# Picking the query rows of each pair of sequences by matrix products instead of by a copy between partitions

## The chip, the core and the metric

The kernel runs on one core of a Trainium2 chip. The metric is the device time of one execution in microseconds (us). The core has a matrix engine (TensorE: PE for products, PEld for its weight loads), VectorE (DVE), ScalarE (ACT), GpSimd (POOL), and queues that issue transfers (DMA), of which SyncE's is SP.

## The reference

A decoder layer for 16 sequences of 56 tokens with 512 features:

```python
x = layernorm(x + mixer(x))              # a state-space mixer: 128 heads of 64, 8 groups
x = layernorm(x + xattn(x, ctx_4096))    # e = softmax(x @ ctx^T); e @ ctx, 1500 keys of 512 per sequence
x = layernorm(x + ffn(x))                # x @ W_base.T + b, and two of eight low-rank experts
```

Only the second and third lines concern us. `xattn` has no projections: the queries are the rows of the first layer norm's output, and the context serves as keys and as values. All of it is in float32.

## The kernel before

The 896 tokens lie packed in `acc`, seven tiles of 128 rows: tile t holds tokens 128t to 128t+127. Up to about 1185 us the mixer runs, group by group. Then comes the attention, which goes by pairs of sequences (`PAIRS` = 8, counted from 0). A pair owns 112 tokens, 112u to 112u+111, which mostly straddle two tiles of `acc`. On the chip a pair is laid out padded: the first sequence on rows 0 to 55, the second on rows 64 to 119, the rows between unused.

The copy `load_x1(u)` (lines 475 to 487, POOL queue) makes that layout: two or three transfers from `acc` into `x1p`, a tile with two slots, whose gaps were zeroed once. `turn_queries(u)` on PE (line 1285) waits for these transfers, transposes the four blocks of 128 features of `x1p` into the PSUM bank `turn` (bank 4) and signals `q_tr`. ACT copies `turn` into `qT` in sixteen pieces (`queries`, line 712). Pair 0 doesn't wait for its transfer: `turn_first_queries` multiplies tile 0 of `acc` by `spread`, an identity with a gap between columns 56 and 64 (line 1298). `x1p` is also the residual that VectorE adds at the end of the pair (`norm2_sum`, line 1036).

I call pass u what PE does in the last loop for u = 0 to 7. In order:

- `score(u)` (line 1392): the products of queries and transposed keys
- `turn_x2(u-1)` (line 1436): transposes of the previous pair's output, which ACT then copies (`x2_evac`, line 724)
- `turn_queries(u+1)` (line 1289)
- `feed_forward(u-1)` (lines 1444 and 1448), which waits for `x2_evac`
- `turn_probs(u)` (line 1463): transposes of the probabilities, which waits for ACT's exponential (line 730)
- `values(u, 0..2)` (line 1477), with `turn_hw` and `lora` (lines 1453, 1457) of the previous pair between them

On DVE a pass has the key transposes of the next pair (`keys_part`, line 934, twelve of them, the first two ahead of `score_max(u)`, line 1022), the routing of the experts and the layer norms. On ACT it has `x2_evac`, `probs_exp`, `router_exp`, eight pieces of `queries(u+1)`, the copies of two thirds of the transposed probabilities into `probsT` (line 736), and the other eight pieces. Each engine executes its list strictly in this order. The context (6 MB per pair) comes through the SP queue into a ring of six units (line 350). A unit is reloaded once the values that read it are done.

`probs` and `probsT` are two tiles of the same shape. `probs_exp(u)` already waits for `z2_done`, that is, for the end of the values of the pair before.

Of the kernel before, what the change touches and what calls it, by code (L numbers as in the profile page):

```python
# [15 lines left out]
f32 = mybir.dt.float32  # L16
f32r = mybir.dt.float32r
ALU = mybir.AluOpType
# [3 lines left out]
P = 128  # L22
# [34 lines left out]
def layer_kernel(nc, A):  # L57
    ctx = ExitStack()
    with ctx:
        def sb(name, shape, dt=f32, stack=ctx):  # L60
            return stack.enter_context(nc.sbuf_tensor(name, shape, dt))
# [8 lines left out]
        acc = sb("acc", [P, TT, DM])  # L70
        ident = sb("ident", [P, P])
        ones = sb("ones", [P, SUB])
# [53 lines left out]
        sq_last = sb("sq_last", [P, TOK], f32, mix)  # L126
        spread = sb("spread", [P, P], f32, mix)
        ssq = sb("ssq", [P, TT], f32, mix)
# [12 lines left out]
        probs = sb("probs", [P, KJ, P], f32, att)  # L141
        probsT = sb("probsT", [P, KJ, P], f32, att)
        x2 = sb("x2", [P, 2, DM], f32, att)
# [14 lines left out]
        for n, k in widths.items():  # L158
# [26 lines left out]
            ss_done ss_picked ss_summed ms_done rg_done outa_done outa_evac outb_done psum_added sum_done  # L185
            wo_high wo_low zeroed y_low_last q0_part spread_set
            residual_loaded residual_set ln1_step ln1_pool ln1_var ln1_rstd x1_set ffn_loaded x1p_zero
# [65 lines left out]
        def x1_landed(u):  # L253

            return 16 * sum(x1_pieces(k) for k in range(u % 2, u + 1, 2))
# [123 lines left out]
        def _(pool):  # L379
            g_ = nc.gpsimd  # L380
            g_.memset(ones[:], 1.0)
            g_.memset(epsc[:], -0.5)
            g_.memset(ident[:], 0.0).then_inc(s["pool_step"], 1)
            g_.memset(causal[:], 1.0)
            g_.memset(causal_hi[:], 1.0).then_inc(s["pool_step"], 1)
            pool.wait_ge(s["pool_step"], 2)
            g_.affine_select(out=ident[:], in_=ident[:], compare_op=ALU.not_equal, fill=1.0, base=0,
                             pattern=[[-1, P]], channel_multiplier=1)
# [4 lines left out]
            last.then_inc(s["consts_set"], 1)  # L393
            g_.memset(spread[:], 0.0).then_inc(s["pool_step"], 1)
            pool.wait_ge(s["consts_set"], 1)
            pool.wait_ge(s["pool_step"], 3)
            for q in range(2):
                last = g_.tensor_copy(spread[:, PAD * q:PAD * q + LEN], ident[:, LEN * q:LEN * (q + 1)])
            last.then_inc(s["spread_set"], 1)
            g_.memset(decay[:].rearrange("p a n -> p (a n)"), 0.0)  # L400
# [361 lines left out]
        def _(dve):  # L762
# [176 lines left out]
            dve.wait_ge(s["zeroed"], 1)  # L939
            v.tensor_reduce(own[:], ident[:].rearrange("p (i a) -> p a i", a=SUB), AX.X, ALU.add)  # L940
            v.tensor_copy(causal[PAD:P, :], causal_hi[PAD:P, :]).then_inc(s["dstep"], 1)
# [49 lines left out]
            keys_part(0, 0, 1)  # L991
            group_squares(GROUPS)
            last_halves(0)
            last_sum(0)
# [156 lines left out]
        def _(pe):  # L1151
# [3 lines left out]
            for k in range(KT):  # L1155
                for r, n in ((0, 4), (1, 3)):
                    i = 2 * k + r
                    for q in range(n):
                        t = 4 * r + q
                        pe.wait_ge(s["h_scaled"], t + 1)  # L1160
                        last = tr([proj[0], proj[1], yt, ob][i // 2][:, i % 2, q * P:(q + 1) * P],
                                  part[:, t, k * P:(k + 1) * P], ident[:])
                    last.then_inc(s["hT_done"], 1)
# [18 lines left out]
            def dt_token_major():  # L1182
                pe.wait_ge(s["dt_dve"], 6)
                for i in range(4):
                    for q in range(4):
                        pair = 4 * (i % 2) + q
                        last = tr([yt, ob][i // 2][:, i % 2, q * P:(q + 1) * P],
                                  (cs_all, dt_all)[i // 2][:, pair * P:(pair + 1) * P], ident[:])
                    last.then_inc(s["cst_done"], 1)
# [5 lines left out]
            def transpose_hid(g, c):  # L1195
                if not within(g, c):
                    return

                wait(pe, s["silu_done"], 10, g, c + 3 if c >= 0 else c + 1)
                wait(pe, s["yres_done"], CT, g, c)  # L1200
                for r in range(2):
                    for q in range(4):
                        pair = 4 * r + q
                        last = tr(yt[:, r, q * P:(q + 1) * P], hid[:, c % 2, pair * P:(pair + 1) * P], ident[:])  # L1204
                    last.then_inc(s["t_done"], 1)
# [178 lines left out]
            last_part(6, 7).then_inc(s["outb_done"], 1)  # L1384
            turn_first_queries()

# [43 lines left out]
            def turn_x2(u):  # L1430
                pe.wait_ge(s["x2_done"], u + 1)
                if u == 0:
                    pe.wait_ge(s["psum_added"], GROUPS * TT)
                at_least(pe, s["hw_evac"], u)
                for k in range(KT):
                    last = tr(misc[:, k * P:(k + 1) * P], x2[:, u % 2, k * P:(k + 1) * P], ident[:])
                last.then_inc(s["x2_tr"], 1)
# [13 lines left out]
            def turn_hw(u):  # L1451
                pe.wait_ge(s["hw_done"], u + 1)
                tr(misc[:, 0:P], hw, ident[:]).then_inc(s["hw_tr"], 1)

# [4 lines left out]
            def turn_probs(u, r):  # L1459
                if r == 0:  # L1460
                    pe.wait_ge(s["exps_done"], u + 1)
                for j in range(KB):
                    last = tr(bank[:, r, j * P:(j + 1) * P], probs[:, KB * r + j, :], ident[:])
                last.then_inc(s["pT_tr"], 1)
# [102 lines left out]
```

## Time and profile before

| | us |
|---|---|
| median of 3 runs | 1479.44 (1477.43 to 1480.03) |
| the profiled execution | 1479.15 |
| its span in the trace | 1477.4 |

| engine | busy us | share of the span |
|---|---|---|
| PE | 1420.3 | 96% |
| PEld | 1169.2 | 79% |
| DVE | 993.2 | 67% |
| ACT | 752.2 | 51% |
| POOL | 496.0 | 34% |

The trace counts from the span's start. Between the two times of the profiled execution lie 1.75 us around the span. Busy shares are means over stages: the mixer fills about four fifths of the span, the attention the last 290 us. Matmuls are pipelined, so the end of one overlaps the start of the next. A float32 product appears as two MATMUL and two LDWEIGHTS records, a transpose as one of each. "[0.51 <-DMA x1p<-acc]" behind a row means that the engine was idle for 0.51 us before it and that this transfer ended the idle time.

### The profile page before, as it was taken

How to read it: one execution, taken by the hardware profiler on the slowest of the kernel's cores; microseconds unless marked ns; L12 is line 12 of the kernel's file. 1: busy time of each engine (PE TensorE's matmuls, PEld its weight loads, DVE VectorE, ACT ScalarE, POOL GpSimd, SP SyncE). 2: the span in 40 equal slices, each digit the busy share in tenths (PEclk: the TensorE clock that was granted, in tenths of full speed). 3: DMA queues.
4: the chain of work that ended last, by engine and by line, in shares of the span. 5: the costliest groups of instructions: out<-in, count | busy, mean ns of one | idle time of the engine just before them, and what ended most of it. 6: DMA issues, size and time to landing. Idle time of an engine off the chain costs nothing.

```text
span 1477.4 us, 30164 instructions
## 1 busy us (share of the span) xinstructions
PE 1420.3 (96%) x12816; PEld 1169.2 (79%) x12816; DVE 993.2 (67%) x1313; ACT 752.2 (51%) x1003; POOL 496.0 (34%) x368
## 2 busy tenths in 40 slices
PE   5899999999999999999999999999999978999995
PEld 4798989898989888888888888889888864445442
DVE  5784768476847684767476757765775676888764
ACT  5765636463756274636463656365536443543340
POOL 5253435242524253425342434333433320111101
PEclk9999999999999999999999999999999999999998
DMA  4431213121312131213221312221221365566610
GB/s 150 118 106 54 82 51 99 47 90 47 98 58 88 40 98 58 81 45 100 65 74 53 97 55 73 58 91 55 73 65 55 131 240 195 217 242 261 195 44 13
DMA packets 53347, 142.60 MB, mean 97 GB/s; under 512 B 9777, under 2 KB 9905, under 8 KB 46951
## 3 DMA queue, kind: packets, MB, share of 16 engines
q1 hardware_dynamic: 51518, 137.01, 28.3%
q0 software_dynamic: 1696, 3.67, 0.8%
q8 instruction: 101, 1.65, 0.5%
q14 instruction: 32, 0.26, 0.0%
HBM read 136.53 MB, written 2.29 MB: 94 GB/s over the span
## 4 chain that ended last, share of the span: by engine, by line
PE 83%; DVE 7%; issue 4%; DMA 3%; ACT 1%; POOL 1%; SPq 0%; DVEq 0%; POOLq 0%; ACTq 0%
PE bank L1174 47%; PE bank L1242 20%; PE bank L1217 5%; PE bank L1204 4%; DVE keysT L934 3%; DMA x1p<-acc 2%; PE bank L1477 2%; PE bank L1392 2%; PE bank L1448 1%; DMA ring_a<-in_context 1%; PE bank L1274 1%; DVE conv L809 1%; PE bank L1229 1%; PE bank L1444 0%; DVE part L770 0%
## 5 line engine op out<-in xcount | busy, mean ns | idle before, releaser
L1174 PE MATMUL bank<-h_hi,w_hi 128*128 128x448 f32 x1152 | 338.2, 375 | 2.2 <-DVE conv L809 2.2
L432 POOL TENSOR_TENSOR y_lo<-yg,y_hi 128x896 fp32r<-128x896 f32 x63 | 134.2, 2129 | 578.6 <-ACT y_hi L605 538.5
L1174 PE MATMUL bank<-h_lo,w_hi 128*128 128x448 f32 x1152 | 328.0, 366 | 0.0
L1174 PE MATMUL bank<-h_hi,w_lo 128*128 128x448 f32 x1152 | 327.1, 365 | 0.0
L809 DVE SCALAR_TENSOR_TENSOR conv<-bank,conv_w,conv 128x880 f32<-128x880 f32 (+2 forms) x240 | 268.0, 1117 | 85.6 <-ACT conv L578 79.8
L1174 PEld LDWEIGHTS bank<-h_hi,w_lo 128*128 128x128 f32 x1152 | 216.8, 188 | 17.4
L1174 PEld LDWEIGHTS bank<-h_lo,w_hi 128*128 128x128 f32 x1152 | 216.9, 188 | 17.2
L416 POOL TENSOR_TENSOR w_lo<-w_raw,w_hi 128x512 fp32r<-128x512 f32 x144 | 188.3, 1308 | 119.1 <-ACT w_hi L544 117.6
L1174 PEld LDWEIGHTS bank<-h_hi,w_hi 128*128 128x128 f32 x1152 | 208.2, 188 | 20.1 <-DVE conv L809 2.6
L854 DVE TENSOR_TENSOR hd_dt<-bank,dt_j 128x512 f32<-128x512 f32 x128 | 82.4, 685 | 208.0 <-PE bank L1204 208.0
L1242 PE MATMUL bank<-wo_hi,y_hi 128*128 128x512 f32 x420 | 165.2, 393 | 0.0
L605 ACT ACTIVATE y_hi<-yg 128x896 fp32r<-128x896 f32 x64 | 60.9, 951 | 203.0 <-DVE yg L836 202.7
L1242 PE MATMUL bank<-wo_lo,y_hi 128*128 128x512 f32 x420 | 163.7, 390 | 0.0
L1242 PE MATMUL bank<-wo_hi,y_lo 128*128 128x512 f32 x420 | 163.4, 389 | 0.0
L585 ACT ACTIVATE hid<-conv 128x896 f32<-128x896 f32 x64 | 61.0, 953 | 150.2 <-DVE conv L809 150.0
L439 POOL TENSOR_TENSOR sqsum<-sq,sqsum 128x896 f32<-128x896 f32 x54 | 115.2, 2133 | 0.0
L578 ACT ACTIVATE conv<-bank,conv_b,conv_w 128x896 f32<-128x896 f32 x80 | 87.1, 1089 | 31.9 <-PE bank L1174 31.7
L1392 PE MATMUL bank<-keysT,qT 32*64 32x384 f32 (+5 forms) x2304 | 90.2, 457 | 9.8 <-issue 6.3
L1242 PEld LDWEIGHTS bank<-wo_hi,y_hi 128*128 128x128 f32 x420 | 78.8, 188 | 19.1 <-issue 2.5
L1242 PEld LDWEIGHTS bank<-wo_hi,y_lo 128*128 128x128 f32 x420 | 78.9, 188 | 16.6
L1392 PEld LDWEIGHTS bank<-keysT,qT 32*64 32x64 f32 x2304 | 59.1, 137 | 41.6 <-issue 27.5
L1242 PEld LDWEIGHTS bank<-wo_lo,y_hi 128*128 128x128 f32 x420 | 78.9, 188 | 15.8
(181 smaller groups left out, 1932.1 us busy)
## 6 DMA issues: line engine op xcount, KB each, us to landing
w_raw<-in_w_in SPq DMA_DIRECT2D x144, 256.0 KB, 2.8
decay<-cs_scratch SPq DMA_DIRECT2D x128, 196.0 KB
ring_a<-in_context SPq DMA_DIRECT2D x24, 1024.0 KB, 7.9
ring_b<-in_context SPq DMA_DIRECT2D x21, 1024.0 KB
wo_raw<-in_w_out SPq DMA_DIRECT2D x64, 256.0 KB, 2.6
ring_b<-in_context SPq DMA_DIRECT2D x3, 896.0 KB
acc<-in_x SPq DMA_DIRECT2D x1, 1792.0 KB, 8.5
out<-z POOLq DMA_DIRECT2D x16, 112.0 KB, 2.7
```

The source lines that it names most:

```text
L416: g_.tensor_tensor(w_lo[:, slot, :], w_raw[:, slot, :], w_hi[:, slot, :].bitcast(f32), ALU.subtract).then_inc(s["w_low"], 1)
L432: g_.tensor_tensor(y_lo[:, c % 4, :], yg[:, c % 2, :], y_hi[:, c % 4, :].bitcast(f32), ALU.subtract).then_inc(s["y_low"], 1)
L439: g_.tensor_tensor(out=sqsum[:], in0=sq[:], in1=sqsum[:], op=ALU.add).then_inc(s["sqsum_done"], 1)
L578: a(seqs(conv[:, m % 2, :]), bank_seqs(proj[idx % 2]), ACT.Identity, bias=conv_b[:, bass.ds(col, 1)], scale=conv_w[:, bass.ds(col, 1), TAP ...
L585: a(real(dst), seqs(conv[:, m % 2, :]), ACT.Silu).then_inc(s["silu_done"], 1)
L605: a(y_hi[:, c % 4, :], yg[:, c % 2, :], ACT.Copy).then_inc(s["y_high"], 1)
L809: v.scalar_tensor_tensor(out=dst[:, :, sh:LEN], in0=src[:, :, 0:LEN - sh], scalar=conv_w[:, bass.ds(col, 1), TAPS - 1 - sh], in1=dst[:, :, ...
L854: v.tensor_tensor(hd_dt[:, 4 * r:4 * r + 4, :].rearrange("p q (h d) -> p q h d", h=2), yt[:, r, :].rearrange("p (q h d) -> p q h d", q=4, ...
L1174: last = mm(place, w[:, k * P:(k + 1) * P], x[:, k, half * HALF:(half + 1) * HALF], start=(k == 0 and i == 0), stop=(k == KT - 1 and i == 2))
L1217: last = mm(yt[HD * h:HD * (h + 1), b, pair * PAD:pair * PAD + LEN], hd_dt[own_rows, pair, HD * h:HD * (h + 1)], mixw[own_rows, h, pair, : ...
L1242: last = mm(ob[:, b, :], y[:, c, tok], w[:, c, :], start=(c == 0 and i == 0), stop=(c == 3 and i == 2))
L1392: last = mm(scores[PAD * q:PAD * (q + 1), row, :].rearrange("p (j i) -> p j i", i=SQ)[:, j0:j1, 0:n], qT[lo:lo + SQ, b // 4, b % 4, PAD * ...
```

## The change

The queries of every pair are now made as those of pair 0 were: by products of the tiles of `acc` with 0/1 columns. A wide tile `shifted` holds zeros with the identity in columns 128 to 255. A strip of 112 of its columns that starts 128 + 112u - 128t columns in picks, from tile t, the rows that belong to pair u. A pair that straddles two tiles (pairs 1 to 6) needs two products per block of features, summed in PSUM; pairs 0 and 7 need one. The output goes to columns 0 to 55 and 64 to 119 of each block of `turn`, and the columns between are zeroed once by VectorE. PE waits for `x1_set` (the tiles' layer norm) and no longer for the transfers. The transfers stay, for the residual. `spread` goes away, and `ident` becomes a slice of `shifted`. `probsT` becomes another name for `probs`, so that the transposed probabilities overwrite those that they were made from.

```diff
-        ident = sb("ident", [P, P])
+        shifted = sb("shifted", [P, 2 * P + 2 * LEN])
+        ident = shifted[:, P:2 * P]
...
-        spread = sb("spread", [P, P], f32, mix)
...
-        probsT = sb("probsT", [P, KJ, P], f32, att)
+        probsT = probs
...
-            g_.memset(ident[:], 0.0).then_inc(s["pool_step"], 1)
+            g_.memset(shifted[:], 0.0).then_inc(s["pool_step"], 1)
...
-            g_.memset(spread[:], 0.0).then_inc(s["pool_step"], 1)
-            pool.wait_ge(s["consts_set"], 1)
-            pool.wait_ge(s["pool_step"], 3)
-            for q in range(2):
-                last = g_.tensor_copy(spread[:, PAD * q:PAD * q + LEN], ident[:, LEN * q:LEN * (q + 1)])
-            last.then_inc(s["spread_set"], 1)
...
             group_squares(GROUPS)
+            v.memset(turn.rearrange("p (a i) -> p a i", i=PAD)[:, :, LEN:PAD], 0.0).then_inc(s["turn_zero"], 1)
             last_halves(0)
...
             def turn_queries(u):
-                pe.wait_ge(x1_loaded[u % 2], x1_landed(u))
-                pe.wait_ge(s["q_set"], u)
+                first, end = 2 * LEN * u, 2 * LEN * (u + 1)
+                tiles = range(first // P, (end - 1) // P + 1)
+                pe.wait_ge(s["x1_set"], tiles[-1] + 1)
+                at_least(pe, s["q_set"], u)
+                if u == 0:
+                    pe.wait_ge(s["turn_zero"], 1)
                 for k in range(KT):
-                    last = tr(turn[:, k * P:(k + 1) * P], x1p[:, u % 2, k * P:(k + 1) * P], ident[:])
-                last.then_inc(s["q_tr"], 1)
-
-            def turn_first_queries():
-                pe.wait_ge(s["x1_set"], 1)
-                pe.wait_ge(s["ss_picked"], GROUPS)
-                pe.wait_ge(s["spread_set"], 1)
-                for k in range(KT):
-                    last = mm(turn[:, k * P:(k + 1) * P], acc[:, 0, k * P:(k + 1) * P], spread[:],
-                              start=True, stop=True)
+                    place = turn[:, k * P:(k + 1) * P].rearrange("p (q i) -> p q i", i=PAD)[:, :, 0:LEN]
+                    for t in tiles:
+                        at = P + first - t * P
+                        last = mm(place, acc[:, t, k * P:(k + 1) * P],
+                                  shifted[:, at:at + 2 * LEN].rearrange("p (q i) -> p q i", i=LEN),
+                                  start=(t == tiles[0]), stop=(t == tiles[-1]))
                 last.then_inc(s["q_tr"], 1)
...
-            turn_first_queries()
+            turn_queries(0)
```

## Rows read from the trace of the kernel before

**Rows 1.** Page, part 4: the chain that ended last, by engine and line.
```profile
PE 83%; DVE 7%; issue 4%; DMA 3%; ACT 1%; POOL 1%; SPq 0%; DVEq 0%; POOLq 0%; ACTq 0%
```

**Rows 2.** What waited for tile x1p, from its own view: us, times.
```profile
  PE bank L1289: 7.5, 6
```

**Rows 3.** Timeline of pass 4: start, length, engine, line, what, idle before.
```profile
1342.03 0.42 PEld L1436 LDWEIGHTS bank<-ident,x 128*128 128x128 f32 x4 [0.60 <-issue]
...
1342.73 0.60 ACT L724 ACTIVATE x2T<-bank 128x512 f32<-128x512 f32 x1 [7.93 <-PE bank L1436]
1343.32 0.42 PEld L1289 LDWEIGHTS bank<-ident,x1p 128*128 128x128 f32 x4 [0.87 <-DMA x1p<-acc]
...
1343.71 1.00 PEld L1444 LDWEIGHTS bank<-waT,x2T 128*128 128x128 f32 x8
...
1343.96 1.54 ACT L730 ACTIVATE probs<-bank,smalls 128x1536 f32<-128x1536 f32 x1 [0.64 <-DVE smalls L1022]
...
1348.18 1.47 PE L1463 MATMUL bank<-ident,probs 128*128 128x128 f32 x12
```

**Rows 4.** Timeline, weight loads of `turn_queries` in passes 2, 3, 5 and 6.
```profile
1282.85 0.42 PEld L1289 LDWEIGHTS bank<-ident,x1p 128*128 128x128 f32 x4 [0.51 <-DMA x1p<-acc]
...
1313.00 0.42 PEld L1289 LDWEIGHTS bank<-ident,x1p 128*128 128x128 f32 x4 [0.84 <-DMA x1p<-acc]
...
1373.16 0.42 PEld L1289 LDWEIGHTS bank<-ident,x1p 128*128 128x128 f32 x4 [0.68 <-DMA x1p<-acc]
...
1406.06 0.42 PEld L1289 LDWEIGHTS bank<-ident,x1p 128*128 128x128 f32 x4 [1.86 <-DMA x1p<-acc]
```

**Rows 5.** Timeline of pass 6, then of pass 7, which turns no queries.
```profile
1403.77 0.42 PEld L1436 LDWEIGHTS bank<-ident,x 128*128 128x128 f32 x4 [0.60 <-issue]
...
1406.44 1.00 PEld L1444 LDWEIGHTS bank<-waT,x2T 128*128 128x128 f32 x8
...
1434.80 0.65 PE L1436 MATMUL bank<-ident,x 128*128 128x128 f32 x4
...
1436.14 1.19 PE L1444 MATMUL bank<-waT,x2T 128*128 128x136 f32 x8 [0.69 <-ACT x2T L724]
```

**Rows 6.** Timeline: the products that pick pair 0's queries.
```profile
1193.67 1.05 PE L1298 MATMUL bank<-spread,acc 128*128 128x128 f32 x8
```

**Rows 7.** Timeline of pass 1.
```profile
1243.94 0.66 PE L1436 MATMUL bank<-ident,x 128*128 128x128 f32 x4
...
1248.49 1.11 PE L1289 MATMUL bank<-ident,x1p 128*128 128x128 f32 x4 [3.90 <-DMA x1p<-acc]
...
1250.63 2.37 DVE L934 STREAM_TRANSPOSE keysT<-ring_a 128x1024 f32<-128x1024 f32 x2 [12.24 <-DMA ring_a<-in_context]
...
1254.68 1.54 ACT L730 ACTIVATE probs<-bank,smalls 128x1536 f32<-128x1536 f32 x1 [9.45 <-DVE smalls L1022]
...
1256.37 1.54 PE L1463 MATMUL bank<-ident,probs 128*128 128x128 f32 x12 [0.40 <-ACT probs L730]
...
1262.01 3.65 PE L1477 MATMUL bank<-ring_b,probsT 125*64 125x512 f32 x16 [0.42 <-ACT probsT L736]
```

**Rows 8.** PE by stretches of pass 1: length, busy (x), granted clock, DMA share, GB/s.
```profile
1244.60:1248.50 3.90, 0.01 (x1) 0.77 1.02 333
1248.50:1253.50 5.00, 5.00 (x15) 0.50 1.01 418
1253.50:1256.00 2.50, 2.48 (x6) 0.99 1.01 413
```

**Rows 9.** The same view for the idle stretch of pass 0.
```profile
1218.20:1221.00 2.80, 0.00 (x0) 1.00 0.00 0
```

**Rows 10.** Timeline around the added VectorE memset: a like one, and the idle time that covers it.
```profile
1189.54 0.75 DVE L923 SCALAR_TENSOR_TENSOR acc<-part,rg,acc 128x512 f32<-128x512 f32 x1 [1.06 <-POOL rg L444]
...
1193.36 0.09 DVE L999 MEMSET bank<- 128x36 f32 x1
```

**Rows 11.** Timeline of the start: PE's first work.
```profile
11.86 1.57 PE L1161 MATMUL bank<-ident,part 128*128 128x128 f32 x4 [11.86 <-DVE part L770]
```

More of the change, by code:

```diff
@@ L185, in layer_kernel @@
             ss_done ss_picked ss_summed ms_done rg_done outa_done outa_evac outb_done psum_added sum_done
-            wo_high wo_low zeroed y_low_last q0_part spread_set
+            wo_high wo_low zeroed y_low_last q0_part turn_zero
             residual_loaded residual_set ln1_step ln1_pool ln1_var ln1_rstd x1_set ffn_loaded x1p_zero
@@ L386, in _ @@
             pool.wait_ge(s["pool_step"], 2)
-            g_.affine_select(out=ident[:], in_=ident[:], compare_op=ALU.not_equal, fill=1.0, base=0,
+            g_.affine_select(out=ident, in_=ident, compare_op=ALU.not_equal, fill=1.0, base=0,
                              pattern=[[-1, P]], channel_multiplier=1)
@@ L939, in _ @@
             dve.wait_ge(s["zeroed"], 1)
-            v.tensor_reduce(own[:], ident[:].rearrange("p (i a) -> p a i", a=SUB), AX.X, ALU.add)
+            v.tensor_reduce(own[:], ident.rearrange("p (i a) -> p a i", a=SUB), AX.X, ALU.add)
             v.tensor_copy(causal[PAD:P, :], causal_hi[PAD:P, :]).then_inc(s["dstep"], 1)
@@ L1161, in _ @@
                         last = tr([proj[0], proj[1], yt, ob][i // 2][:, i % 2, q * P:(q + 1) * P],
-                                  part[:, t, k * P:(k + 1) * P], ident[:])
+                                  part[:, t, k * P:(k + 1) * P], ident)
                     last.then_inc(s["hT_done"], 1)
@@ L1187, in dt_token_major @@
                         last = tr([yt, ob][i // 2][:, i % 2, q * P:(q + 1) * P],
-                                  (cs_all, dt_all)[i // 2][:, pair * P:(pair + 1) * P], ident[:])
+                                  (cs_all, dt_all)[i // 2][:, pair * P:(pair + 1) * P], ident)
                     last.then_inc(s["cst_done"], 1)
@@ L1203, in transpose_hid @@
                         pair = 4 * r + q
-                        last = tr(yt[:, r, q * P:(q + 1) * P], hid[:, c % 2, pair * P:(pair + 1) * P], ident[:])
+                        last = tr(yt[:, r, q * P:(q + 1) * P], hid[:, c % 2, pair * P:(pair + 1) * P], ident)
                     last.then_inc(s["t_done"], 1)
@@ L1435, in turn_x2 @@
                 for k in range(KT):
-                    last = tr(misc[:, k * P:(k + 1) * P], x2[:, u % 2, k * P:(k + 1) * P], ident[:])
+                    last = tr(misc[:, k * P:(k + 1) * P], x2[:, u % 2, k * P:(k + 1) * P], ident)
                 last.then_inc(s["x2_tr"], 1)
@@ L1452, in turn_hw @@
                 pe.wait_ge(s["hw_done"], u + 1)
-                tr(misc[:, 0:P], hw, ident[:]).then_inc(s["hw_tr"], 1)
+                tr(misc[:, 0:P], hw, ident).then_inc(s["hw_tr"], 1)
             def lora(u):
@@ L1462, in turn_probs @@
                 for j in range(KB):
-                    last = tr(bank[:, r, j * P:(j + 1) * P], probs[:, KB * r + j, :], ident[:])
+                    last = tr(bank[:, r, j * P:(j + 1) * P], probs[:, KB * r + j, :], ident)
                 last.then_inc(s["pT_tr"], 1)
```

## The prediction

> **What bounds the kernel now.** I read the page's chain first: 83% of the time that sets the end is PE and 3% are transfers [rows 1]. So a microsecond added to PE's list is likely to show, and the transfers can give back little. Next I asked the view of tile x1p who waits for the copy that the change takes out of PE's way. PE waits 7.5 us in all, six times [rows 2]. That is the most the removed wait can return. The timeline shows where the six waits lie: 3.90 us in pass 1 [rows 7], 0.5 to 0.9 us in each of passes 2 to 5 [rows 3, 4], 1.86 us in pass 6 [rows 4]. (The idle times of the weight loader are slightly longer than those of the products, and I use them, since the load comes first.) The transfer itself takes some 7 us, but the scores of the pass, about 10.6 us, run beside it. Only its tail is seen.
>
> Then comes the question for each wait: what is late next once it is gone? It has three different answers, so I take the passes apart.
>
> **A product's price.** The old turn is four transposes. From its first weight load to the first of the feed-forward it takes 0.39 us (1343.32 to 1343.71 in pass 4, [rows 3]). The new turn of a straddling pair is 8 float32 products, each with two records, so 16. The nearest row is the pick of pair 0, the same operation with 128 columns: 8 records in 1.05 us, of which the last one takes 0.275 us, so they start (1.05 - 0.275)/7 = 0.111 us apart [rows 6]. With 112 columns I scale by 112/128 to 0.097. 16 records take 1.6 us (0.100 each, with a little for the strided output). The bounds are 16 x 0.0955 = 1.53 if only the columns count, and 16 x 0.111 = 1.78 if the weight load sets the pace, which doesn't shrink with the columns.
>
> The Trainium skill speaks against the change here. "TensorE: Matmul & The Clock Gate", section "Terms", says that the transpose mode makes float32 four times faster. The trace disagrees: the twelve transposes of the probabilities take 1.47 us, that is (1.47 - 0.27)/11 = 0.109 us each [rows 3], against 0.222 us for a product [rows 6], a factor of two. By the page, a product of 112 columns would take 4 x 0.109 x 7/8 = 0.38 us and eight of them 3.05 us. What that would give stands under the first rival.
>
> **Passes 2 to 5: slower.** PE is the path here. The probabilities' transposes start right behind the feed-forward, without idle time, and the exponential that they need was done 2.7 us before, at 1345.5 [rows 3]. VectorE and ACT wait for PE in these passes. The turn and the wait before it cost 0.39 + idle: with 0.51, 0.84, 0.87 and 0.68 us idle [rows 3, 4] that is 0.90, 1.23, 1.26 and 1.07. The new turn takes 1.6 each time and needs nothing that is late: its tiles' norms were finished a pass or more before. The differences are +0.70, +0.37, +0.34 and +0.53, in sum **+1.9 us** (+1.7 at 1.53, +2.7 at 1.78). Less than nothing is excluded, because the feed-forward also waits for ACT's copy of x2 (1342.73 + 0.60 [rows 3]), 1.34 us after the transposes of x2 start. The products cover all of that, so there is no gain beyond what I counted.
>
> **Pass 6: faster.** It turns pair 7, which lies in one tile: 4 products, 0.8 us. From the transposes of x2 to the feed-forward it took 1406.44 - 1403.77 = 2.67 us. Pass 7, which turns nothing, shows what is late next: 1436.14 - 1434.80 = 1.34 us, set by ACT's copy [rows 5]. 0.42 + 0.8 fits under it. The gain is **-1.3 us**. The later work of that pass is PE's alone, so I keep it whole (bounds -1.3 and 0).
>
> **Pass 1: no gain, and probably a loss.** PE waited 3.90 us for x1p, but afterwards it waits again, for the exponential, at 1256.37. The exponential follows the row maximum, which on VectorE stands behind the first key transposes of the next pair, and these waited 12.24 us for the context's transfer, until 1250.63 [rows 7]. The change moves none of that. PE finishes earlier and waits longer: turn at 1244.36, +1.6, feed-forward 4.47 us as in pass 4 (1343.71 to 1348.18 [rows 3]), end at 1250.4. Then it is idle 5.9 us at a stretch, where there were 3.9 and later 0.4.
>
> What an idle spell costs is in the clock. After the 3.9 us idle spell the granted clock was 0.50 (1.2 of 2.4 GHz) for the next 5.0 us of work, then full again; 0.77 within the spell means that it fell 1.8 us before the work resumed, 6.8 us in all [rows 8]. Before, this slow stretch lay on work that had time, ahead of the wait for the exponential. Now the idle spell lies right ahead of work that has none. 5.0 us at half speed do 2.5 us of work too little. The second part of the values stood idle for ACT for 0.42 us [rows 7], which absorbs as much: 2.5 - 0.4 gives **+2.1 us**. The bounds are 0, if the clock holds, and 6.8/2 - 0.4 = 3.0, if the whole slow stretch falls on this work. A gain is excluded by VectorE's order. The rule of the skill's same page, section "Why this matters for your kernels", is that an idle gap between bursts of products drops the array to half its clock. Here the trace agrees (0.50 after 3.9 us).
>
> **The rest, costed at nothing.** Pass 0: the turn of pair 1 is 1.1 us longer, ahead of an idle stretch of 2.8 us [rows 9]. Without that cover it would be +1.1. Pair 0's pick has 112 columns instead of 128, 0.1 us less, and the scores behind it wait for key transposes anyway. VectorE's memset of 64 columns (like one of 36, 0.09 us) stands ahead of `last_halves(0)`, and what follows that idles 1.06 us for POOL [rows 10]. Uncovered it would cost 0.1. At the start POOL clears 368 columns instead of 128, and PE starts only at 11.86, for VectorE [rows 11]. Only a clearing that takes microseconds longer would be seen. POOL's memset and two copies of `spread` go, ahead of a wait that POOL has anyway. The single buffer for the probabilities adds no wait: each third is overwritten after its own transposes, for which the copies waited already, and the next exponential waited already for the end of the values. The new waits of PE (`x1_set`, `turn_zero`) have the whole PE list queued behind them, but are set long before: `turn_zero` some 5 us before the pick, since VectorE is past it at 1189.54 [rows 10].
>
> **Sum.** 1.9 - 1.3 + 2.1 = +2.7 us on the profiled execution's 1479.15 gives **1481.9 us** (1481.85). That execution is 0.29 us below the median of 1479.44, so against the median it is +2.4 us, 0.16%. A measurement of this kernel tells about 0.2%, 3.0 us, from no change. The forecast's own range is 1479.15 + 0 + 1.7 - 1.3 = 1479.5 to 1479.15 + 3.0 + 2.7 - 1.3 = 1483.6, or 1484.9 without the gain of pass 6.
>
> **Rivals.**
> - *Products at the price of their weight load (slower).* If a record takes about 0.19 us, the turn takes 3.05 us. This happens if loads of different contents don't overlap the products when these are short. Passes 2 to 5 then cost 12.2 - 4.46 = +7.7, pass 6 gains only 2.67 - (0.42 + 1.5) = 0.7, pass 1 stays at +2.1: 1488.3 us. The sum passes 0.2% from 0.105 us a record (4 x 16 x 0.105 - 4.46 - 1.3 + 2.1 = 3.1); up to 0.111 that is the forecast's own upper half, beyond it this rival. Against it stands the 0.111 of the same operation [rows 6]. For it stands that no row has fewer than 128 columns with full weights of this type. It is also the time that the skill's factor of four gives.
> - *Pass 1's wait was real (faster).* If the context for pair 2 usually lands before about 1247, the exponential is ready when PE is, and the 3.9 us count. The sum is 1.9 - 1.3 - 3.9 = -3.3, 1475.9 us. Against it: the transfer landed at 1250.63 with the DMA share at 1.0 [rows 7, 8], and VectorE would have to gain 4 us.
> - *The clock holds in pass 1 (no change).* After 2.8 us idle in pass 0 the clock stayed at 1.00 [rows 9]. Where it holds, only 1.9 - 1.3 = +0.6 is left: 1479.8 us. Against it: 5.9 us idle is twice that and longer than the 3.9 that brought it down [rows 8].
>
> **How the numbers follow.** Forecast 0.6; of this 0.38 within 0.2% and 0.22 above, since 1482.1 is within its range. Load price 0.08, slower. Real wait 0.1, faster. Clock holds 0.2, of which 0.18 is within 0.2% and 0.02 slower. The last 0.02 is any other gain or loss, half each. Faster 0.11, same 0.56, slower 0.33. The range leaves out most of the faster and of the load-price case and holds the rest with its bounds: 1477.5 to 1486.0.
>
> **What would show it.** In the changed kernel's timeline: in passes 2 to 5 some 1.6 us of picking products and no idle time before them (a longer turn: first rival); 2.0 us from x2's transposes to the feed-forward, against 1.34 to 1.68; in pass 6, 1.34; in pass 1 an idle PE from about 1250.4 to 1256.4 with the exponential as releaser, and a granted clock of 0.50 after it (1.00: third rival; no idle time: second). The forecast is wrong if the passes are no longer bound by PE, or if stalls inside the scores move.

## The result and the profile after

| | before | after |
|---|---|---|
| median of 12 runs | 1479.40 us (1475.14 to 1480.79) | 1483.16 us (1481.86 to 1486.81) |
| ratio, 95% interval | 1 | 1.003 (1.0022 to 1.0038) |
| profiled execution, and its span | 1479.15, 1477.4 | 1483.10, 1481.4 |
| PE's share of the chain | 83% [rows 1] | 91% |
| PE waits for the copy x1p | 7.5 us, 6 times [rows 2] | not at all |

The change makes the kernel 3.8 us slower. The forecast was 1481.9, within 1477.5 to 1486.0. The time lies in the range and 1.3 us above the forecast, and by its interval it is slower rather than "no change", which had the higher chance (0.56 against 0.33). Much of the work below asks which terms of the sum were right and what the 1.3 us are.

The chain of the changed kernel, from its page, against [rows 1]: PE has 8 points more, DVE 3 fewer, the transfers and "issue" 2 fewer each.

```profile
PE 91%; DVE 4%; issue 2%; DMA 1%; ACT 1%; POOL 0%; SPq 0%; DVEq 0%; ACTq 0%
```

Pass 4 of the changed kernel in the timeline (start, length, engine, line, what, idle before), against [rows 3]:

```profile
1344.84 0.66 PE L1431 MATMUL bank<-shifted,x 128*128 128x128 f32 x4
1345.34 1.94 PE L1292 MATMUL bank<-shifted,acc 128*128 128x112 f32 x16
1345.54 0.60 ACT L718 ACTIVATE x2T<-bank 128x512 f32<-128x512 f32 x1 [8.11 <-PE bank L1431]
1347.11 1.11 PE L1439 MATMUL bank<-waT,x2T 128*128 128x136 f32 x8
```

The wait is gone. In its place stand 16 product records. ACT's copy of x2 is done at 1345.54 + 0.60 = 1346.14, so the feed-forward at 1347.11 waits for the products and for nothing else. It starts 2.27 us after the transposes of x2 instead of 1.79. The 16 records take 1.77 us of the chain (start, length, what):

```profile
1345.50 1.77 PE bank L1292 x16
```

Pass 6 of the changed kernel, against [rows 5]. Eight records stand there, and then a stall that waits for no semaphore:

```profile
1406.03 0.66 PE L1431 MATMUL bank<-shifted,x 128*128 128x128 f32 x4
1406.52 1.04 PE L1292 MATMUL bank<-shifted,acc 128*128 128x112 f32 x8
1406.72 0.60 ACT L718 ACTIVATE x2T<-bank 128x512 f32<-128x512 f32 x1 [16.43 <-PE bank L1431]
1409.12 1.09 PE L1439 MATMUL bank<-waT,x2T 128*128 128x136 f32 x8 [1.56 <-issue]
```

Pass 1 of the changed kernel, against [rows 7]:

```profile
1248.00 0.93 PE L1292 MATMUL bank<-shifted,acc 128*128 128x112 f32 x7 [0.89 <-issue]
...
1249.71 3.60 PE L1443 MATMUL bank<-wbT,x2T 128*128 128x512 f32 x8
...
1251.15 2.37 DVE L928 STREAM_TRANSPOSE keysT<-ring_a 128x1024 f32<-128x1024 f32 x2 [11.23 <-DMA ring_a<-in_context]
...
1255.20 1.54 ACT L724 ACTIVATE probs<-bank,smalls 128x1536 f32<-128x1536 f32 x1 [8.44 <-DVE smalls L1017]
...
1256.88 2.82 PE L1458 MATMUL bank<-shifted,probs 128*128 128x128 f32 x12 [3.58 <-ACT probs L724]
```

and PE by stretches of it (length, busy (x), granted clock, DMA share, GB/s), against [rows 8]:

```profile
1253.30:1256.80 3.50, 0.00 (x1) 0.80 1.00 417
1256.90:1261.80 4.90, 4.90 (x18) 0.50 0.55 226
1262.40:1266.00 3.60, 3.60 (x20) 1.00 0.22 32
```

VectorE's key transposes still wait for the context and the exponential still follows them, so PE's wait of 3.9 us became a wait of 3.6 us further down. The clock that it brings down, 0.50 for 4.9 us, now meets the transposes of the probabilities: 2.82 us instead of 1.54. Before, it met the feed-forward, which had time [rows 7, 8].

The 4.0 us between the two profiled executions, stage by stage. For the passes the numbers are from one start of x2's transposes to the next:

| stage | after - before, us |
|---|---|
| mixer, up to the pick of pair 0 (1193.7 to 1194.5) | +0.8 |
| pass 0, up to the x2 transposes of pass 1 (1243.94 to 1245.47) | +0.7 |
| pass 1 (37.98 to 37.86) | -0.1 |
| passes 2, 3, 4 (29.82, 30.29, 30.04 to 30.53, 30.98, 30.66) | +2.0 |
| pass 5 (31.70 to 30.53) | -1.2 |
| pass 6 (31.03 to 31.34) | +0.3 |
| pass 7 (22.18, both) | 0 |
| behind the last transposes of x2 (20.4 to 21.85) | +1.4 |

One pair of profiles misleads in places, which is why the experiments follow. The last row is the slow stretch of the clock. It comes from the 2.92 us wait ahead of the last x2 transposes, which both kernels have. The tail is 21.7 us in the kernel with only the wait removed (experiment 1, the old turn) and 20.5 in a second profile of the changed kernel (experiment 5), so it varies from profile to profile and belongs to neither. Pass 0's 0.7 us look like that too: after the idle spell ahead of the first scores the same 221 records take 7.98 us before and 8.90 after. But in experiment 5 they take 7.98 and pass 0 is still 0.85 us longer than before, so this row isn't explained. The same eight instructions of the last pair's feed-forward, before and then after:

```profile
1460.30 4.33 PE L1448 MATMUL bank<-wbT,x2T 128*128 128x512 f32 x8
```
```profile
1462.87 5.68 PE L1443 MATMUL bank<-wbT,x2T 128*128 128x512 f32 x8
```

### The profile page after: what moved, and what is told of

Same layout as the page of the kernel before. It is cut to its first block, busy times and chain, and to the rows that moved or that the text cites. A ratio compares the mean times of both kernels' runs of the same rounds, so it can differ in the third digit from the quotient of the medians.

```text
span 1481.4 us, 30313 instructions
## 1 busy us (share of the span) xinstructions
PE 1432.0 (97%) x12892; PEld 1179.2 (80%) x12892; DVE 993.0 (67%) x1314; ACT 753.2 (51%) x1003; POOL 496.1 (33%) x365
## 4 chain that ended last, share of the span: by engine, by line
PE 91%; DVE 4%; issue 2%; DMA 1%; ACT 1%; POOL 0%; SPq 0%; DVEq 0%; ACTq 0%
PE bank L1169 47%; PE bank L1237 20%; PE bank L1387 5%; PE bank L1472 5%; PE bank L1212 5%; PE bank L1199 4%; PE bank L1443 2%; DMA ring_a<-in_context 1%; DVE keysT L928 1%; PE bank L1269 1%; PE bank L1458 1%; DVE conv L803 1%; PE bank L1439 1%; PE bank L1292 1%; PE bank L1224 1%
```

## The experiments

All ratios are against the kernel before on the same chip, with 95% intervals. "x2 to feed-forward" is the time on PE from the start of x2's transposes to the start of the feed-forward, in passes 2 to 5.

**1. The wait alone, without products (`e1_no_wait`).** The kernel before, whose turn transposes a tile of `acc` that is ready, so the queries of the pairs are other rows than they should be. x1p is still loaded. This prices the wait that the change removes.

```diff
-                pe.wait_ge(x1_loaded[u % 2], x1_landed(u))
+                tile = min(u, TT - 1)
+                pe.wait_ge(s["x1_set"], tile + 1)
...
-                    last = tr(turn[:, k * P:(k + 1) * P], x1p[:, u % 2, k * P:(k + 1) * P], ident[:])
+                    last = tr(turn[:, k * P:(k + 1) * P], acc[:, tile, k * P:(k + 1) * P], ident[:])
```

> The kernel before, but the turn of pairs 1 to 7 transposes a tile of acc instead of x1p, so PE has no transfer to wait for and still pays the old 0.39 us for the turn. (The queries of these pairs are other rows than the reference's.) This is the removed wait alone. Theory: passes 2 to 5 fall to the 1.34 us that ACT's copy of x2 sets (0, -0.3, -0.3, -0.1), pass 6 gains 1.3 us, and pass 1 loses about 1.9 us, because its idle spell moves to just ahead of the probabilities' transposes and they and the first values run at a granted clock of 0.50. Sum -0.2 us, ratio 0.9999. Rival 'pass 1's wait was real': -6 us, ratio 0.996. Rival 'the clock in pass 1 costs nothing': -2.1 us, ratio 0.9986.

Measured: 1478.05 us, 0.9989 (0.9978 to 1.0). Of 7.5 us of waiting, 1.1 us came back, and the interval just reaches "nothing". x2 to feed-forward is 1.35 us (before: 1.43, 1.76, 1.79, 1.58), in pass 6 1.34. In pass 1 it is 1.34 too, instead of 5.46, and that gain is gone by the exponential. Its timeline:

```profile
1246.11 1.19 PE L1445 MATMUL bank<-waT,x2T 128*128 128x136 f32 x8 [0.25 <-ACT x2T L724]
...
1256.03 2.82 PE L1464 MATMUL bank<-ident,probs 128*128 128x128 f32 x12 [5.30 <-ACT probs L730]
```

and its stretch behind that (length, busy (x), granted clock, DMA share, GB/s):

```profile
1256.10:1260.90 4.80, 4.80 (x18) 0.50 0.47 196
```

So pass 1's wait was covered, and its removal costs by the clock, products or not. From the end of the exponential to the scores of pass 2 it is 14.28 us before, 16.10 after and 16.23 here.

**2. The products behind the old wait (`e2_products_after_wait`).** The changed kernel, whose products also wait for the copy, as the transposes did. x1p is loaded in the changed kernel anyway.

```diff
+                if u:
+                    pe.wait_ge(x1_loaded[u % 2], x1_landed(u))
```

> The changed kernel, but PE again waits for the transfer of x1p before the products. This is the price of the products alone. Theory: 1.77 us for a straddling pair instead of 0.39 in passes 2 to 5 (+5.5 us), +0.5 us in pass 6, and in pass 1 about +2 us, since 16 records at half clock end after the exponential is ready. Sum about +8 us against the kernel before, ratio 1.0054. Rival 'the products cost little, and what the changed kernel lost lies in stalls elsewhere': +2 to +4 us, ratio 1.002.

Measured: 1487.59 us, 1.0054 (1.0034 to 1.0074). x2 to feed-forward is 2.81, 3.28, 2.95 and 2.99 us, against 2.27, 2.26, 2.27 and 2.26 without the wait. With the wait kept, the change costs 8.5 us, without it 3.8 and 4.9 (the changed kernel and experiment 5), so removing the wait returns some 4 us of what the rest of the change costs. PE doesn't read x1p in this kernel, so the profile puts its six waits for the copy down to "issue" (8.4 us in all). In pass 1 the products run beside the slow clock: 16 of them take 3.73 us. The probabilities' transposes then follow without idle time:

```profile
1250.28 3.73 PE L1294 MATMUL bank<-shifted,acc 128*128 128x112 f32 x16 [3.87 <-issue]
...
1258.97 1.47 PE L1460 MATMUL bank<-shifted,probs 128*128 128x128 f32 x12
```

**3. The single buffer for the probabilities, alone (`e3_one_buffer`).**

```diff
-        probsT = sb("probsT", [P, KJ, P], f32, att)
+        probsT = probs
```

> The kernel before with one buffer for the probabilities and nothing else. Theory: every wait that it needs was there already, so nothing changes: ratio 1.000, within 0.15%, and the same length of passes 2 to 5 (29.8 to 30.3 us, 31.7 with a stall). Rival 'reading and overwriting the same tile costs': some 0.5 us a pass, +4 us, ratio 1.0027.

Measured: 1480.74 us, 1.0007 (0.9997 to 1.0016). The interval holds 1, and no new wait stands in its passes. It costs nothing that can be told.

**4. The same wait removed another way: the transfer issued earlier (`e4_issue_first`).** The kernel before. POOL issues the load of x1p ahead of the norm of the pair before instead of behind it.

```diff
-                if u >= 1:
-                    rstd2(u - 1)
                 if 1 <= u < PAIRS - 1:
                     load_x1(u + 1)
+                if u >= 1:
+                    rstd2(u - 1)
```

> The kernel before, but POOL issues the transfer of x1p for the next pair ahead of the power for the second layer norm, not behind it, about 1.7 us earlier. Transposes and transfer stay. Theory: the waits of passes 2 to 5 (0.5 to 0.9 us) go down to what ACT's copy of x2 needs, pass 6 gains up to 1.3 us, pass 1 gains nothing: -2.1 us, ratio 0.9986. Rival 'the landing follows the context's traffic and not the issue': less than 1 us, ratio 0.9995 to 1.000.

Measured: 1478.57 us, 0.9993 (0.9984 to 1.0002). The waits all but go: x2 to feed-forward is 1.35, 1.34, 1.64, 1.35, in pass 6 1.34, in pass 1 1.42. Everything that the removal of the wait can bring is in this edit, without one product. The total doesn't tell from no change.

**5. The changed kernel again (`e5_after_again`), for a second profile.**

> The changed kernel once more, beside the next one. Theory: ratio 1.0025 to 1.003. A second profile tells which parts of the first one's passes repeat: 30.5 to 31.0 us for passes 2 to 5, about 16 us from the probabilities' transposes of pass 1 to the scores of pass 2 (14.1 in the kernel before), and PE's stalls of 0.9 and 1.6 us that the profile puts down to issue.

Measured: 1484.08 us, 1.0037 (1.0024 to 1.005). From the end of pass 1's exponential to the scores of pass 2 it is 15.15 us, between the 14.28 of before and the 16.10 of the first profile. x2 to feed-forward is 2.26 or 2.27 in each of passes 2 to 5, and stalls without a semaphore stand again in passes 1 and 6 (1.45 and 1.84 us). Passes 5 and 6 take 31.17 and 31.62 us. The idle spell ahead of the probabilities' transposes of pass 1 is 3.18 us here.

**6. Keeping PE busy in pass 1's idle spell, six products (`e6_fill_idle`).** The changed kernel. Products whose result nobody reads stand between the feed-forward and the wait for the exponential.

```diff
+                if u == 1:
+                    pe.wait_ge(s["z2_done"], 1)
+                    for _ in range(6):
+                        mm(pv, shifted[:, P:2 * P], acc[:, 0, :], start=True, stop=True)
```

> The changed kernel with six float32 products of 512 columns (0.43 us each, result unused) between the feed-forward and the probabilities' transposes of pass 1, so that TensorE works through most of the spell in which it waits for the exponential. Theory (the clock's fall behind the moved idle spell costs 1.9 us): granted clock 1.00 after it, 14.1 us from those transposes to the scores of pass 2, and 1.9 us less in all than the changed kernel, ratio 1.0015 to the kernel before. Rival (the clock there costs nothing, pass 1 is longer for another reason): as the changed kernel, 1.0028, or more by whatever the added products delay.

Measured: 1483.6 us, 1.0036 (1.0022 to 1.005). I had mis-sized the filling: a float32 product of 512 columns is two records, 0.86 us and not 0.43. The twelve records ran past the end of the exponential and pushed the transposes back by 1.35 us. But these then ran at full speed:

```profile
1252.34 5.31 PE L1491 MATMUL bank<-acc,shifted 128*128 128x512 f32 x12
...
1257.49 1.47 PE L1458 MATMUL bank<-shifted,probs 128*128 128x128 f32 x12
```

From the end of the exponential to the scores it is 14.74 us, 1.35 of them the overshoot.

**7. Products of half the columns (`e7_56_columns`).** The changed kernel, which picks only the first sequence of each pair; the queries of the second one are zero. If columns set the price of a product, this one falls.

```diff
...
-                    place = turn[:, k * P:(k + 1) * P].rearrange("p (q i) -> p q i", i=PAD)[:, :, 0:LEN]
+                    place = turn[:, k * P:(k + 1) * P].rearrange("p (q i) -> p q i", i=PAD)[:, 0:1, 0:LEN]
...
-                                  shifted[:, at:at + 2 * LEN].rearrange("p (q i) -> p q i", i=LEN),
+                                  shifted[:, at:at + LEN].rearrange("p (q i) -> p q i", i=LEN),
...
```

> The changed kernel, but the picking products have 56 moving columns instead of 112 and fill only the first sequence of each pair. (The second sequence's queries are zero.) Row 'weight load sets the pace': the records stay 0.11 us apart and the turn of a straddling pair stays 1.77 us. Row 'columns set the pace': about 0.05 us apart and 0.8 us.

Measured, in a single run: 1483.28 us. The chain of pass 4:

```profile
1343.98 1.73 PE bank L1292 x16
```

1.73 us for 16 records, against 1.77 with 112 columns: 0.108 against 0.111 each. Half the columns take 2% off. It isn't the moving columns that set the pace.

**8. The early transfer with three spells filled (`e8_early_transfer_filled`).** Experiment 4, with unused products of 512 columns ahead of the first scores (7), in pass 1 (9) and ahead of the last x2 transposes (6).

```diff
+            def fill(place, n):
+                for _ in range(n):
+                    mm(place, ident[:], acc[:, 0, :], start=True, stop=True)
...
+                fill(bank[:, 0, :], 7)
...
+                if u == 1:
+                    pe.wait_ge(s["z2_done"], 1)
+                    fill(pv, 9)
...
+            pe.wait_ge(s["pT_evac0"], PAIRS)
+            fill(bank[:, 0, :], 6)
```

> The kernel before with the transfer issued first (as in the earlier run) and unused float32 products of 512 columns in three idle spells of TensorE: seven ahead of pair 0's scores, nine ahead of the probabilities' transposes of pass 1, six ahead of the last pair's transposes of x2. Theory (idle spells cost through the clock behind them): -0.8, -0.6 and -1.8 us for the spells and -1 to -2 for the earlier transfer, ratio 0.9965. Rival (the clock behind idle spells lies on work that has time): only what the earlier transfer gives, 0.9993.

Measured: 1481.26 us, 1.0018 (1.0009 to 1.0027). This carried the same error in size: the fillings take 6.17, 7.89 and 5.31 us, and each one runs past what PE would have waited for. It says nothing against filling, only what filling too much costs.

**9 and 10. The place in memory (`e9_before_moved`, `e10_after_moved`).** The profiles had shown something that no theory of mine held: all kernels built on the changed one reach the pick of pair 0 some 2 us later than experiments 1, 3 and 4, although nothing in the mixer is changed. What differs is where its tiles lie. The strips make a tile ahead of them 960 bytes wider in each partition. So one kernel is the one of experiment 3 with such a gap (its `probsT = probs` isn't repeated in the cut), the other the changed kernel with 64 bytes more, 1024 in all.

```diff
         ident = sb("ident", [P, P])
+        gap = sb("gap", [P, 2 * P + 2 * LEN - P])
```
```diff
         ident = shifted[:, P:2 * P]
+        gap = sb("gap", [P, 16])
```

> The kernel before with one buffer for the probabilities and an unused tile of 240 columns behind ident, so that every tile of the mixer lies 960 bytes further on, as in the changed kernel. No instruction differs from the one-buffer run. In all five profiles of kernels with the changed kernel's code a group of the mixer takes 144.85 us, in the others 144.5 us. Theory (the tiles' place in memory does it): 144.85 us a group here too, the picks of pair 0 at 1194 to 1195 us instead of 1192.5, ratio 1.002. Rival (something in the changed kernel's instructions does it, the identity as a slice of a wider tile among them): 144.5 us a group, ratio 1.0005.

> The changed kernel with an unused tile of 16 columns behind the wide identity, so that the mixer's tiles lie 1024 bytes further on than before instead of 960. Theory of place, if multiples of 1024 bytes count alike: 144.5 us a group, 2.3 us less than the changed kernel, ratio 1.001 to 1.0015. Rival: 144.85 us a group and ratio 1.003, as the changed kernel; then either the distance that counts is another or the place does not count, which the run before this one tells.

Measured: 1480.88 us, 1.0008 (0.9999 to 1.0017), and 1483.7 us, 1.0021 (1.0011 to 1.0031). The total that the theory gave for the first, 1.002, lies above its interval; the second's interval holds both of its expectations. The mixer's period is the time between two starts of its first product of a group. In the timelines, first experiment 3, then the same with the gap of 960 bytes:

```profile
467.22 1.15 PE L1229 MATMUL bank<-cmat,bmat 128*64 128x56 f32 x32
...
611.77 1.15 PE L1229 MATMUL bank<-cmat,bmat 128*64 128x56 f32 x32
```
```profile
468.03 1.15 PE L1230 MATMUL bank<-cmat,bmat 128*64 128x56 f32 x32
...
612.87 1.15 PE L1230 MATMUL bank<-cmat,bmat 128*64 128x56 f32 x32
```

144.55 us and 144.84. Then the changed kernel, and the changed kernel with 1024 bytes instead of 960:

```profile
467.95 1.15 PE L1224 MATMUL bank<-cmat,bmat 128*64 128x56 f32 x32
...
612.79 1.15 PE L1224 MATMUL bank<-cmat,bmat 128*64 128x56 f32 x32
```
```profile
466.78 1.15 PE L1225 MATMUL bank<-cmat,bmat 128*64 128x56 f32 x32
...
611.32 1.15 PE L1225 MATMUL bank<-cmat,bmat 128*64 128x56 f32 x32
```

144.84 us and 144.54. The gap alone slows the mixer of the kernel without the change, and 64 bytes more undo it in the changed one. Up to the end of the mixer that is some 2.0 to 2.5 us: pair 0 is picked at 1192.5 in experiment 3, 1194.5 with the gap, 1194.5 in the changed kernel, 1192.0 with 1024 bytes. The kernel before was picked at 1193.7 only because its first group began 1.5 us late in the profiled execution, so the table above shows 0.8 where other pairs of profiles show about 2. The chain over one group says which products are slower, the kernel of experiment 3 first, then with the gap:

```profile
602.11 9.73 PE bank L1174 x48
```
```profile
603.02 9.92 PE bank L1175 x48
```

Two of a group's 18 projections stand in this piece. They and one more take 0.4133 us for each two records instead of 0.4055, the others don't change. The slower mixer is shown by the period, which is 144.5 to 144.6 in all seven profiles without the 960 bytes (that with 1024 among them) and 144.8 to 144.9 in all seven with them. Why an address matters for just three of eighteen is open.

That these 2 us reach the end isn't shown. Between experiments 3 and 9 they are gone at the first transposes of x2, 50 us behind the pick:

```profile
1245.32 0.66 PE L1436 MATMUL bank<-ident,x 128*128 128x128 f32 x4
```
```profile
1245.38 0.66 PE L1437 MATMUL bank<-ident,x 128*128 128x128 f32 x4
```

Their ratios are 1.0007 and 1.0008. The ratio of experiment 10 is 0.0009 below the changed kernel's, some 1.3 us, with overlapping intervals. In its profile PE reaches the x2 transposes of pass 2 at 1280.23 us, 3.1 us before the changed kernel, and those of pass 7 at 1437.76, 0.4 us behind it. Most of that lead is lost in pass 6, by a stall longer than the 1.56 us of the changed kernel and a granted clock of 0.57 in the 4 us from 1408:

```profile
1407.83 1.53 PE L1440 MATMUL bank<-waT,x2T 128*128 128x136 f32 x8 [2.12 <-issue]
```

**11. The filling, four products (`e11_fill_four`).** Experiment 6 with `range(4)`.

> The changed kernel with four unused products in pass 1 instead of six. A float32 product of 512 columns took 0.86 us, two records of 0.43, so that six held PE 1.35 us beyond the exponential. Four take 3.4 us and end before it. Theory (clock): 1.00 behind it, 14.2 us from the end of the exponential to the scores of pass 2 against 16.1 in the changed kernel, and 1.9 us less in all, ratio 1.0015 to 1.002. Rival (the clock's spell moves on to later work): as the changed kernel, 1.003.

Measured: 1483.85 us, 1.0028 (1.0018 to 1.0038). The timeline, and PE in the stretch where the clock was 0.50 (length, busy (x), granted clock, DMA share, GB/s):

```profile
1251.56 3.60 PE L1491 MATMUL bank<-acc,shifted 128*128 128x512 f32 x8
...
1256.32 1.53 PE L1458 MATMUL bank<-shifted,probs 128*128 128x128 f32 x12 [1.17 <-ACT probs L724]
```
```profile
1256.50:1260.00 3.50, 3.47 (x22) 1.00 0.74 307
```

The clock stays at 1.00, and from the end of the exponential to the scores it is 14.27 us, against 16.10 in the changed kernel: 1.8 us, which is the clock's term. The total shows nothing of that gain. In its profile pass 6 has a longer stall and a longer period (33.64 us instead of 31.34):

```profile
1407.44 1.37 PE L1292 MATMUL bank<-shifted,acc 128*128 128x112 f32 x8 [2.18 <-issue]
```

Experiments 6 and 10 lose as much there (under "Pass 6" below); whether every run does isn't settled by single profiles.

**12. The early transfer with fillings that fit (`e12_early_transfer_filled2`).** Experiment 8 with 3, 4 and 3 products.

> The early transfer with unused products again, now three, four and three of 0.86 us instead of seven, nine and six, so that they end before what PE waits for. Theory: nothing is delayed, the granted clock is 1.00 behind the filled spells, and the last pair's feed-forward takes 4.5 us instead of 5.5 to 6.6. With the early transfer that makes -3 to -4 us against the kernel before, ratio 0.9975. Rival (the clock behind idle spells lies on work that has time): 0.9993, as the early transfer alone.

Measured: **1475.51 us, 0.9973 (0.9963 to 0.9984)**, faster than both kernels. Pass 1, then the last pass:

```profile
1254.59 1.53 PE L1468 MATMUL bank<-ident,probs 128*128 128x128 f32 x12 [0.54 <-ACT probs L730]
...
1449.02 2.74 PE L1399 MATMUL bank<-acc,ident 128*128 128x512 f32 x6
...
1454.47 3.60 PE L1453 MATMUL bank<-wbT,x2T 128*128 128x512 f32 x8
```

The eight records that took 4.33 us before and 5.68 after take 3.60. The tail behind the last x2 transposes is 19.5 us instead of 20.4. The filling ahead of the first scores brought nothing that its profile shows: in pass 0 the probabilities' transposes take 2.82 us, at a granted clock of 0.50, against 1.53 before.

## Why the prediction came out as it did

**The waits and what hid them: right.** Pass 1's 3.90 us were covered by the transfer of the context. The rival of a real wait (1475.9 us) falls twice: in the changed kernel the exponential stands 0.5 us later than before (1255.20 against 1254.68), and in experiment 1 the wait's removal alone brings 1.1 us, not 3.9 and more.

**A product's price: the mechanism right, the value too low.** The sum took 0.100 us a record, scaled by the columns, with 0.111 as the upper bound "if the weight load sets the pace". It is 0.111 (1.77/16), and experiment 7 shows that the columns indeed don't matter here: 0.108 with 56. The row of the same operation [rows 6] held the right number unscaled. The rival of 0.19 a record falls: 16 records don't take 3.05 us. With it falls, for these shapes, the factor of four of the Trainium skill ("TensorE: Matmul & The Clock Gate", section "Terms"): a product of two records takes 0.222 us and a transpose 0.109.

**Passes 2 to 5: +1.9 forecast, +2.5 measured.** x2 to feed-forward is 9.06 us in sum against 6.56. The difference of 0.6 is the price: 4 x 16 x 0.011 = 0.7. The upper bound of 2.7 held.

**Pass 6: -1.3 forecast, +0.3 measured.** The eight products fit under ACT's copy as worked out. But behind them stands the stall of 1.56 us, so 1.34 us became 3.09. The step that fails is "what is late next is ACT's copy". It holds where no products stand: in experiments 1, 4 and 12 pass 6 has 1.34 or 1.35 us. In the six profiles with the products and without the wait it has 3.09 to 4.71. The kernel before has such stalls too, elsewhere, 0.68 us in the scores ahead of pass 2 and 1.03 in those ahead of pass 6. In its timeline:

```profile
1401.68 2.16 PE L1392 MATMUL bank<-keysT,qT 32*64 32x384 f32 x43 [1.03 <-issue]
```

In the changed kernel this one is gone, and pass 5, in whose scores it stood, is 1.2 us shorter. Passes 5 and 6 together take 0.9 us less than before. With pass 5's products at +0.5 the forecast has -0.8 for the two. So in this profile the gain was there, in another pass. In experiment 5 it was not: 62.79 us against 62.73 before. In the other kernels built on the changed one without the wait the two passes take even more, 65.27, 64.00, 64.69 and 65.09 us (experiments 6, 7, 10 and 11), so the gain can't be counted on. The stall keeps its place in PE's list of instructions: it stands behind the eight products of the turn in the changed kernel, ahead of them in experiment 11, which has eight records more ahead of it, and behind the first of x2's four transposes in experiment 6, which has twelve more. The prediction named this at its end ("if stalls inside the scores move") but put no price on it.

**Pass 1: +2.1 forecast, +1.8 measured in the profile of the changed kernel (0.9 in experiment 5).** The idle spell was 3.6 us and not the 5.9 of the forecast, since the pass began 1.5 us later and stalled for 0.9. Even so the clock fell to 0.50 behind it and took 1.8 us, and experiments 6 and 11 show that it is the idle spell: with PE kept busy in it the clock stays at 1.00 and the 1.8 us are back in that stretch. The rival "the clock holds" falls. The Trainium skill, "TensorE: Matmul & The Clock Gate", section "Why this matters for your kernels", states the rule that an idle gap between bursts of products brings the clock down to half, and these runs agree with it in pass 1. In the period of pass 1 none of this shows (37.86 against 37.98), because the pass began 1.5 us later while the context landed only 0.5 us later, which takes off 1.0, and a stall of 0.68 us in the scores ahead of pass 2 was not there.

**The rest at nothing: right for pass 0's turn and the single buffer, wrong for the mixer.** Pass 0 has the products under its idle stretch, of which 1.55 us are left, and the probabilities' transposes stand 1.52 us later than before, just as much as the turn ahead of them does (1219.01 against 1217.49):

```profile
1219.01 2.04 PE L1292 MATMUL bank<-shifted,acc 128*128 128x112 f32 x16
...
1222.59 1.53 PE L1458 MATMUL bank<-shifted,probs 128*128 128x128 f32 x12 [1.55 <-ACT probs L724]
```

One step isn't in the prediction at all: a wider tile moves every tile behind it, and in this kernel that is the mixer's, 80% of the span. It costs 2 us up to the pick of pair 0, of which the totals of experiments 3 and 9 show nothing at the end. It was costed at nothing by not being looked at, and no row of the kernel before could have told its size.

**The sum.** The cleanest split is by kernels. Experiment 9 has the single buffer and the tiles' place of the changed kernel with the old turn, and takes 1.0008 of the time before; the changed kernel takes 1.003. So what the products cost, less what the wait gave back, is 0.0022, some 3.3 us, uncertain by about 1.8 (both intervals together). The forecast had 2.7 for it. Passes 2 to 5 are the part that repeats: their feed-forward comes 2.26 or 2.27 us behind the transposes of x2 in both profiles of the changed kernel. That the forecast of 2.7 comes so near is partly luck: passes 5 and 6 didn't give the gain it had, and pass 1 lost less than it had. The other 1.2 us of experiment 9, the single buffer and the place together, can't be told from nothing.

The other terms don't add up one by one. Experiment 10 takes the mixer's 2 us away and experiment 11 the clock's 1.8, and the totals fall by 0.0009 and 0.0002, 1.3 and 0.3 us, within the noise. In their profiles the time comes back later. From the x2 transposes of pass 2 to those of pass 7 it is 157.5, 157.3 and 157.1 us in experiments 10, 11 and 6, which start at 1280.2, 1281.0 and 1281.7, but 154.0 in the changed kernel, which starts at 1283.3 (156.0 in experiment 5, which starts at 1284.8; 152.9 in the kernel before). What these passes wait for, so that a lead is lost in them, stays open.

## What to carry to other kernels

A removed wait is worth what stands behind it, pass by pass: here 7.5 us of waiting held 0.5 to 1.1 us (experiments 4 and 1, both hardly told from nothing), an earlier issue of the transfer takes the wait away without any new work, and the products that replaced the transfer stand on the engine that bounds the kernel. Scale a float32 product of up to 128 columns by its records, not by its columns. When a tile changes its size, compare the period of the hot loop behind it, even if no instruction there is changed, and then follow the difference to the end of the kernel: a lead can be lost again at the next stall. When an idle spell stays, ask whether work or unused products that end before the awaited event keep the clock for what follows.

## What the runs showed of the hardware

- Float32 products with full 128 x 128 weights have the same price at 56, 112 and 128 columns: 0.108, 0.111 and 0.111 us a record. Transposes of the same size take 0.109.
- A shift of the mixer's tiles by 960 bytes made 3 of 18 projections 2% slower (0.4133 against 0.4055 us for two records), and one by 1024 bytes didn't. The cause wasn't found.
- PE stalls for 0.2 to 2.2 us without a semaphore in the passes whose context is being loaded, at a DMA share near 1.0. These stalls stand mainly in pass 5's scores with the old turn (0.54 to 1.41 us in experiments 3, 4, 1, 9 and the kernel before) and around pass 6's turn with the products (1.56 to 2.18 us in six profiles), and they move with the number of records ahead of them. In pass 0 two of them stand exactly 128 records apart in the kernel before, 0.98 and 3.61 us long. That PE waits for its next instructions beside the context's transfers would fit, but no run tested it.
- Two idle spells of the same length cost differently by what follows. 3.9 us ahead of the feed-forward cost nothing, 3.6 us ahead of the probabilities' transposes cost 1.8 us. And a wait of 2.9 us ahead of the same transposes in pass 0 left the clock at 1.00 in the kernel before, but they ran at 0.50 behind the same wait in experiments 1 and 9, 2.82 us instead of 1.53. Ten unused products, in 3, 4 and 3, together with the earlier transfer made the kernel 0.27% faster; 22 of them made it 0.18% slower.
